# Attention with a mixture-of-experts feed-forward on one core: row maxima issued by a table, and other units for the small work

## The reference, cut to what matters

```python
x = x + tanh(g_xattn) * xattn(layernorm(x), ctx, ctx)      # scores * 0.125, softmax over 1601 keys
x = x + tanh(g_ffn) * moe(layernorm(x))                    # 8 experts, top 2 per token
```

## Time and profile before

| | |
|---|---|
| median of 3 runs | 1453.89 us (1453.78 to 1454.77) |
| profiled execution | 1453.8 us, span 1452.0 us |
| PE, DVE, ACT, POOL busy, share of the span | 94%, 81%, 76%, 38% |
| first window of maxima, first score | 25.7 us, 46.2 us |
| attention ends, first expert matmul | 1259.6 us, 1264.3 us |

### The profile page before, as it was taken

How to read it: one execution, slowest core, us unless ns; L and a number is a source line. 1 busy time by engine, 2 the same in 40 slices (tenths; PEclk the granted TensorE clock), 3 DMA queues, 4 the chain that set the end, 5 groups by cost and what they waited for, 6 DMA issues and landing times.

```text
span 1452.0 us, 37914 instructions
## 1 busy us (share of the span) xinstructions
PE 1357.7 (94%) x13936; PEld 643.2 (44%) x13936; DVE 1175.5 (81%) x2300; ACT 1102.6 (76%) x2202; POOL 549.6 (38%) x1214
## 2 busy tenths in 40 slices
PE   4699999999999999999999999999999999899992
PEld 2134444444343444443434343434343444488882
DVE  6578898989898989898998989898989899355334
ACT  1278888888888888888888888888888888765551
POOL 2241535252534353534434343435252511145442
PEclk7599999999999999999999999999999999999996
DMA  4321121212120212121211212121211110276665
GB/s 138 91 79 56 37 69 39 72 34 77 31 81 25 71 38 67 46 62 51 57 57 53 60 52 62 49 63 45 67 40 47 38 46 2 67 228 208 197 196 207
DMA packets 65540, 109.15 MB, mean 75 GB/s; under 512 B 13436, under 2 KB 36348, under 8 KB 65212
## 3 DMA queue, kind: packets, MB, share of 16 engines
q1 hardware_dynamic: 56572, 91.64, 21.4%
q0 software_dynamic: 4544, 9.45, 1.9%
q10 hardware_dynamic: 4240, 5.65, 1.3%
HBM read 48.81 MB, written 14.64 MB: 44 GB/s over the span
## 4 chain that ended last, share of the span: by engine, by line
PE 61%; DVE 25%; SPq 5%; issue 3%; DMA 2%; POOL 2%; ACTq 0%; ACT 0%; POOLq 0%; DVEq 0%
DVE mx L1437 20%; PE pv L738 20%; PE mxp L717 11%; PE st L695 10%; PE st L968 5%; PE mxp L976 5%; SPq L364 4%; PE st L797 3%; PE st L806 3%; PE st L817 1%; DMA arena<-results 1%; PE st L840 1%; DMA qpack<-mxT 1%; PE mxp L947 1%; PE mxp L955 1%
## 5 line engine op out<-in xcount | busy, mean ns | idle before, releaser
L1437 DVE TENSOR_REDUCE mx<-mxp 128x2 f32<-128x804 f32 x1024 | 982.9, 988 | 126.2 <-PE mxp L717 113.7
L1005 ACT ACTIVATE arena<-st 128x512 f32<-128x512 f32 (+1 forms) x1664 | 897.9, 594 | 124.3 <-PE st L695 114.3
L738 PE MATMUL pv<-arena 128*32 128x256 f32 x6656 | 536.0, 394 | 0.5
L695 PE MATMUL st<-qpack,kpack 51*128 51x256 bf16 (+1 forms) x3328 | 464.4, 274 | 11.6 <-ACT kf L1036 8.9
L717 PE MATMUL mxp<-kpack,qpack 48*128 48x402 bf16 x2048 | 437.8, 345 | 34.5 <-DVE mx L1437 30.6
L695 PEld LDWEIGHTS st<-qpack,kpack 51*128 51x128 bf16 (+1 forms) x3328 | 209.5, 97 | 166.6 <-ACT arena L1005 56.2
L717 PEld LDWEIGHTS mxp<-kpack,qpack 48*128 48x128 bf16 x2048 | 128.0, 94 | 252.9 <-DVE mx L1437 136.2
L738 PEld LDWEIGHTS pv<-arena 128*32 128x32 f32 x6656 | 132.7, 109 | 178.0 <-issue 119.5
L1147 ACT ACTIVATE arena<-st,bias 128x256 f32<-128x256 f32 x156 | 73.6, 473 | 63.6 <-PE st L968 60.9
L633 POOL DMA_INDIRECT results<-ysb,idx x78 | 74.7, 957 | 93.4 <-DVE ysb L1576 80.3
L968 PE MATMUL st<-xT,arena 128*128 128x256 f32 x312 | 95.7, 390 | 4.5 <-issue 2.6
(11 more groups left out here) (182 smaller groups left out, 1075.0 us busy)
## 6 DMA issues: line engine op xcount, KB each, us to landing
kpack<-ksp SPq DMA_DIRECT2D x762, 50.0 KB
arena<-in_ctxT SPq DMA_DIRECT2D x14, 800.5 KB, 4.5
arena<-in_w1T SPq DMA_DIRECT2D x39, 256.0 KB
arena<-in_w2T SPq DMA_DIRECT2D x39, 256.0 KB
qpack<-qsp SPq DMA_DIRECT2D x186, 32.0 KB
xblk<-rows SPq DMA_DIRECT2D x39, 132.0 KB, 2.8
rows<-in_pads SPq DMA_DIRECT2D x8, 264.0 KB, 3.7
qpack<-mxT SPq DMA_DIRECT2D x128, 3.0 KB
```

The source lines that it names most:

```text
L695: ins = eng.matmul(ring[i][0:n, jj * N:(jj + 1) * N], kpack[rows, b % 2, g * JJ + jj, kt * P:kt * P + n], qpack[rows, b % 2, g * JJ + jj, ...
L738: ins = eng.matmul(pv[32 * j:32 * j + 32, 0:N], vaug[0:n, b % 2, kt, VC * h:VC * h + 32], pt[0:n, (2 * u + rg) % PT_BUFS, jj * N:(jj + 1) ...
L1005: eng.activation(pt[0:n, c % PT_BUFS, :], ring[bank_of["S", u, p]][0:n, :], ACT.Exp, scale=SCALE).then_inc(s_exp, 1)
L1437: eng.tensor_reduce(mx[:, tj, w, :], mxp[windows_done % MX_BUFS][:, :, 0:WIN], AX.X, ALU.max).then_inc(s_red, 1)
```

## The change

Windows of maxima are issued by a written table: `WINDOWS_AT` says for each of the 52 units how many stand in the scores (first string, 35) and at the end (second string, 29), 64 a batch as before. The windows run 29 ahead (before 27), but only 20 are issued ahead of the first score (before 22), and the lead is made up over the first 27 units. `small` goes by the unit: routing has one step a unit from r = 29 (before two steps at each of ten maxima), the X norm has one step at the end of each of the units 28 to 32, the L norm one in each of 11 to 15. Nearly all units of the tables move. At the start POOL's memset of the whole of `vaug` goes; DVE sets the columns of ones and the padding instead. SP packs group 2 of batch 0 ahead of `place_maxima(0)`, and ACT's queue packs group 3. POOL splits the maxima of groups 3 and 4 ahead of what stood before them.

```diff
-AHEAD = KT + 9
-SHORT = 4
-K_AT = {2: 0, 5: 1, 10: 2, 11: 3}
-V_AT = {19: 0, 20: 1, 28: 2, 32: 3}
-HEADS_AT, TURN_AT, PLACE_AT = {4: 0, 18: 1, 31: 2, 44: 3}, {8: 1, 22: 2, 34: 3, 48: 4}, {9: 1, 23: 2, 35: 3, 49: 4}
-POST_AT = {7: "C", 9: "F", 24: "L", 27: "R"}
-X_AT, Q_AT = 36, 42
-X1_AT, Q1_AT = 4, 7
-RANK_AT, LAST_RANK_AT, COUNT_AT, PLAN_AT = 43, 40, 42, 44
+K_AT = {1: 0, 3: 1, 7: 2, 11: 3}
+V_AT = {14: 0, 26: 1, 27: 2, 32: 3}
+HEADS_AT, TURN_AT, PLACE_AT = {2: 0, 22: 1, 29: 2, 41: 3}, {8: 1, 21: 2, 34: 3, 47: 4}, {9: 1, 22: 2, 35: 3, 48: 4}
+POST_AT = {6: "C", 10: "F", 23: "L", 25: "R"}
+X_AT, Q_AT = 36, 40
+X1_AT, Q1_AT = 4, 6
+RANK_AT, LAST_RANK_AT, COUNT_AT, PLAN_AT = 46, 35, 38, 40
+L_NORM_AT, X_NORM_AT = 11, 28
+LOGITS_AT, EXP_AT, ROUTE_AT = 26, 28, 29
+LEAD, SHORT = 29, 9
+WINDOWS_AT = ("1101110001111100111001011111011010011111010011110111",
+              "0110012110100120001111100111010011100001111000110000")
...
+def issued(u, p):
+
+    b, r = divmod(u, UNITS)
+    return LEAD + b * PER_BATCH + ISSUED[2 * r + p] - max(0, SHORT - u // 3)
...
@@ SP
+            pack_keys(0, 2)
             place_maxima(0)
-            for g in range(2, NG):
-                pack_keys(0, g)
@@ POOL
             norm("X", 0)
-            eng.memset(vaug, 1.0).then_inc(s_vone, 1)
             split_maxima(0)
...
+                split_maxima(b * NG + 3)
                 if b + 2 < B:
                     norm("X", b + 2)
-                split_maxima(b * NG + 3)
+                if b + 1 < B:
+                    split_maxima(b * NG + 4)
                 if b > 0:
                     count_first(b - 1)
@@ ACT
             eng.dma_start(ctx_sb[:, 1, :], ctxT[1]).then_inc(s_ctx[1], 16)
+            for part in range(PARTS):
+                for rg in range(RG):
+                    pack_key_rows(eng, 0, NG - 1, part, rg)
@@ DVE
-            def small(b, w):
+            def small(b, r, p):
+
+                if p == 1:
+                    if b + 2 < B and X_NORM_AT <= r < X_NORM_AT + 5:
+                        norm_step("X", b + 2, r - X_NORM_AT)
+                    return
...
+                each = 4 if last else 1
+                first = r - (rank_at(b) + 1)
...
+                for n in range(each * (r - ROUTE_AT), each * (r + 1 - ROUTE_AT)):
+                    if 0 <= n < 20:
+                        routing_step(b - 1, n)
...
+            eng.memset(vaug[:, :, :, 0:VC * H].rearrange("p k t (h c) -> p (k t) h c", c=VC)[:, :, :, DH], 1.0
+                       ).then_inc(s_vone, 1)
+            eng.memset(vaug[:, :, :, VC * H:VW].rearrange("p k t w -> p (k t) w"), 0.0).then_inc(s_vone, 1)
...
-            for v in range(AHEAD - SHORT):
-                for p in range(RG):
-                    for w in windows(v, p):
-                        maximum(*w)
-                if KT <= v:
-                    norm_step("X", 1, v - KT)
+            for n in range(issued(0, 0)):
+                maximum(*divmod(n, NMX))
+            for n in range(5):
+                norm_step("X", 1, n)
...
+                for w in windows(u, 0):
+                    maximum(*w)
+                small(b, r, 0)
...
+                for w in windows(u, 1):
+                    maximum(*w)
+                small(b, r, 1)
```

More of the change, by code:

```diff
@@ L86 @@
 N_W2 = 4
-K_AT = {2: 0, 5: 1, 10: 2, 11: 3}
-V_AT = {19: 0, 20: 1, 28: 2, 32: 3}
-HEADS_AT, TURN_AT, PLACE_AT = {4: 0, 18: 1, 31: 2, 44: 3}, {8: 1, 22: 2, 34: 3, 48: 4}, {9: 1, 23: 2, 35: 3, 49: 4}
-POST_AT = {7: "C", 9: "F", 24: "L", 27: "R"}
-X_AT, Q_AT = 36, 42
-X1_AT, Q1_AT = 4, 7
-RANK_AT, LAST_RANK_AT, COUNT_AT, PLAN_AT = 43, 40, 42, 44
-SLOTS = GROUPS * NMX // B
+K_AT = {1: 0, 3: 1, 7: 2, 11: 3}
[10 more added lines that the diff above has]
+              "0110012110100120001111100111010011100001111000110000")
+PER_BATCH = NG * NMX
+ISSUED = [sum(int(WINDOWS_AT[q][r]) for r in range(UNITS) for q in range(2) if 2 * r + q < c)
+          for c in range(2 * UNITS)]
 def key_rows(kt):
     return min(P, M - kt * P)
+def issued(u, p):
+    b, r = divmod(u, UNITS)
+    return LEAD + b * PER_BATCH + ISSUED[2 * r + p] - max(0, SHORT - u // 3)
 def windows(u, p):
[L103 to L113, removed]
+    to = issued(u, 1) if p == 0 else issued(u + 1, 0)
+    return [divmod(n, NMX) for n in range(issued(u, p), min(to, GROUPS * NMX))]
 def rank_at(b):
@@ L891, in _ @@
                 b, r = divmod(u, UNITS)
-                first = [w for v in beside(u) for w in windows(v, 0)]
-                scores(u, 0, first[:1])
+                scores(u, 0, windows(u, 0)[:1])
                 scores(u, 1, [])
-                for w in first[1:]:
+                for w in windows(u, 0)[1:]:
                     maximum(*w)
@@ L931, in _ @@
                     count_tokens(0)
-                for v in beside(u):
-                    for w in windows(v, 1):
-                        maximum(*w)
+                for w in windows(u, 1):
+                    maximum(*w)
             for v in range(B * UNITS - LAG, B * UNITS):
@@ L1126, in _ @@
                             copy_tokens(b - 1)
-                    if r == 31:
+                    if r == EXP_AT:
                         exp_logits(b - 1)
@@ L1411, in take_full @@
                                              ALU.min).then_inc(s_dve, 1)
-            def small(b, w):
-                last = b == B - 1
[L1416 to L1424, removed]
+            def small(b, r, p):
[3 more added lines that the diff above has]
+                    return
+                if b == 0:
+                    return
+                last = b == B - 1
+                each = 4 if last else 1
+                first = r - (rank_at(b) + 1)
+                if L_NORM_AT <= r < L_NORM_AT + 5:
+                    norm_step("L", b - 1, r - L_NORM_AT)
+                elif LOGITS_AT <= r < LOGITS_AT + 2:
+                    logit_step(b - 1, r - LOGITS_AT)
+                for n in range(each * (r - ROUTE_AT), each * (r + 1 - ROUTE_AT)):
+                    if 0 <= n < 20:
                         routing_step(b - 1, n)
[L1426 to L1429, removed]
+                for n in range(1 + each * first, 1 + each * (first + 1)):
+                    if 1 <= n < 5:
+                        place_step(b - 1, n)
             def maximum(G, m):
```

7 lines of the change are left out of this document (2 added, 5 removed).

## The result

The changed kernel takes 1461.56 us in the median of 5 runs (1459.28 to 1462.2), the kernel before 1454.76 beside it (1453.78 to 1457.39): ratio 1.0041 [1.0026, 1.0055], **slower by 0.4%** where 1416 was forecast. The profiled execution has 1459.28 us and a span of 1457.2; that of before had 1452.0.

The account below looks back on a forecast made before the run. PE's unit work was put at 70.8 of 75.05 us a batch, 4.3 being stalls behind close second windows. Gains of 14 (start), 19 (batches 1 to 13), 3.2 and 1.2 summed to 37.4 off 1453.8: 1416 us, range 1388 to 1434.

Parts of the forecast that it names:

- One moved step is late: Steady batch: X norm's last step moves to unit 32, so PE waits 1.8 us for its rows in unit 36.
- rival A: Steady batches: the wait for the X rows does not come, 25 us more gained, 1391 us; chance 0.2.
- (d): Start: with continuous work TensorE stays at 2.4 GHz from about 49 us; about 18.5 gained by unit 9.
- What is left ... I take 1.1: Steady batch: stalls remaining at close second windows, turned maxima and backlog, 1.1 us a batch, bounds 0.5 and 3.
- Rival C: Steady batches: the table paces only half as well, stalls 2.8 instead of 1.1 us, 1440 us; chance 0.09.
- (a): Start: with POOL's memset gone, the packs and the first window come 3.65 us earlier.
- (c): Start, unit 2: ACT's 12.25 us wait for packs, and some 9 us of PE standing with it, go.
- (b): Start: group 2 packs before the first placing, group 3 on ACT; first score at about 42.1 instead of 46.2 us.
- rival B: Start: DMA engines, not issue, set it, so it brings 4, 1426 us; sign: first score after 44; chance 0.1.
- (e): Batch 0: second placing waits for queries ready near 64.4 us, lands at 89; a 4 to 5 us stall, 15.2 remain.
- The last batch: Last batch and hand-over: stalls fall 1.8, hand-over gains 2.3, PE stands 2.9 for divide; net 1.2 gained.
- rival D: Steady batches: X wait of 5 us behind a DVE backlog uses up the gain, 1461 us, slower; chance 0.04.

Follow-up runs that it names:

- e1: Changed kernel with the rows of batch b+2 turned in unit 38, not 36: 1411.87 us, ratio 0.9723 to the kernel before.
- e5: Changed kernel with rows turned in unit 38, plan behind unit 44 and packs of group 2 behind the first placing: 1406.09 us, ratio 0.9679.
- e18: e5 with one window moved from the end of unit 46 to the end of unit 3: 1410.98 us, ratio 0.9719.
- e6: Changed kernel with rows at 38 and the written table replaced by the even pattern from before: 1455.91 us, ratio 1.0011.
- e7: Changed kernel with rows at 38 and routing two steps at a time in units 34 to 43: 1417.66 us, ratio 0.9753.
- e8: Changed kernel with rows at 38 and three start edits (GpSimd memset, VectorE memsets, packs of groups 2 and 3) taken back: 1421.16 us, ratio 0.9771.
- e4: Changed kernel with SyncE's packs of group 2 behind the placing of the first maxima: 1454.42 us, ratio 1.0011.
- e3: Changed kernel with the last batch's plan steps behind unit 44, not 40: 1455.3 us, ratio 1.0014.
- e15: The changed kernel itself, run again in a series with the stand: 1519.56 us, ratio 1.0172.
- e9: Changed kernel with rows turned one unit earlier, in 35: 1570.97 us, ratio 1.0503.
- e11: e5 with one window moved from the end of unit 46 to the end of unit 3: 1492.45 us, ratio 0.9973.
- e12: Changed kernel with rows turned in unit 35, run once more: 1566.05 us, ratio 1.0448.
- e14: e5 with the window of unit 46 moved to unit 3, run again in a series with the stand: ratio 0.994.
- e17: e5 with the window of unit 46 moved to unit 3, in the series of e15: 1488.53 us, ratio 0.9955.
- the three edits: Changed kernel with rows in 38, plan behind 44, packs behind the first placing: 0.9679 as e5; 1486.6 us, 0.9948 in the series with the stand.

## Why the prediction was wrong, by its own steps

**The steady batch, "One moved step is late": this is the step that failed.** Place, releaser, number and length of the wait were right (14 times, 1.87 against 1.8, rival A's 1391 was never near). But the step was priced at the wait alone: "Sum: 70.7 + 1.1 + 1.8 = 73.6". The runs give 1.87 for the wait and, on average, 19.9 / 13 = 1.5 for the stretches at 1.2 GHz behind it, missing from the sum. The text had the low clock as a consequence of stands in batch 0 (step (d) of the start) and didn't carry it to its own new wait, nor to the 2.9 us stand that it put into the last batch. Over 14 batches that is some 21 us of the 45 between forecast and result.

**"What is left ... I take 1.1"** was mis-sized. Without wait a batch takes 72.77 (e1, e5), so stalls are 2.1 on a sum of 70.7 and not 1.1, within the bounds of 0.5 and 3. The two largest are unit 46 (2.41 in e5, against 1.59 by the prediction's own prices) and unit 2 (2.28 against 1.61); the prediction's list has a part of the first and not the second. This is 1.0 in each of 13 batches, 13 us. The first can't be had by moving its window alone (e18); the second was not tried. Rival C (1440) named 2.8, of the right kind but too much. That the even pattern costs 3.0 more (e6) bears out the reading of the earlier trace rows: second windows close behind the first were the stalls. That two routing steps at a time cost much, which the text drew from the 1.19 of the earlier trace rows, does not hold: 0.3 a batch (e7).

**The start** was put at 14 and brings 6 to 7 (mark of batch 1, e8). (a) is right in kind and too large: the memset is gone and the first window runs 2.0 us earlier (23.67 against 25.70), not 3.65. (c) is right: the 12.25 us wait is gone, and back in e8. (b) failed: the first score at 49.4 and not 42.1, because the packs, issued ahead of the placing "where SP waits anyway", were costed at their issue alone, and not at what they hold up behind them; e4 shows it. Against (b) the text had set what the Trainium skill, page "DMA: Bandwidth & Descriptors", section "Issuing engines are not separate DMA queues", says of shared DMA engines, and had chosen the sequencer. Each was right in part: the 12.25 us wait did go, and the first score was later than 44, the sign of rival B. (d) came late, with the full clock from about 55 us and not 49. (e) was too early by 7.8: the queries waited for GpSimd until 72.16, the placing landed at 97.5 and not at 89, and PE stood 0.6 us for it and not 4 to 5, since it was late itself.

**The last batch**: 2.9 us for `divide` were put down, 1.83 are the wait, and with the clock of 0.64 behind it the stretch is 3.4 longer. With the plan at 44 (e3) 3.1 of these come back, but the stretch is still 0.3 above that of before, so the 1.8 forecast from fewer stalls isn't there either. From the last copy to the first expert multiplication it is 2.22 us instead of 4.72: 2.5 gained, 2.3 forecast. That number is luck. The forecast had it from the plan four units earlier, and with the plan back at 44 it is 2.40 (e3) and 2.22 (e5); what does bring it was not tried.

Batch 14 (3.2 against 2.9) was right. Of the chance of 0.05 for slower, 0.04 went to rival D, a wait above 4.5 us. That its 1461 is the measured time is chance: the wait was 1.87 and not 5, and none of what D asks for happened. Its bound was worked out right: 37.4 / 14 + 1.8 a batch. Wait and clock together are 3.4 us a batch; with 8 less at the start, 1.0 more of stalls a batch and 2.5 less at the end, that was enough.

## What to carry to other kernels

A new wait of TensorE is priced with what the clock does behind it: here 0.8 and 1.25 us cost no more than themselves, 1.87 us cost 1.5 more on average, and 2.9 us 2.3 to 2.6 more; so work out each wait that an edit adds to some tenths, and move the consumer by a unit before the producer is tuned. A small transfer that something waits for goes ahead of the bulk, even where the queue would stand idle meanwhile: here that was 5.8 us at the first score and 3.6 behind batch 0. And where the stalls that are left all go back to one engine that is busy nine tenths of the time, moving the work that shows a stall may only move the stall.

## What the runs showed of the hardware that was not expected

- TensorE's clock fell to 1.2 GHz behind 11 of 14 stands of 1.87 us in an otherwise busy stream, and behind none of 14 at 0.8 and of 13 at 1.25. Which of the 14 keep it differs from trace to trace: the same waits in e3, e4 and e15 have the fall 12, 11 and 7 times, in other batches. The times of e3 and e4 spread over 13 and 17 us in 12 runs each, but those of the changed kernel itself over 3 in 5, so the spread alone shows little.
- In three series (e9 to e11, e12 to e14, e15 to e17) PE, ScalarE and VectorE stop together in unit 1 of each batch, where GpSimd scatters rows and SP packs queries. In e11 the unit takes 5.73 us (671.14 to 676.87; 1.94 in e5), and the releaser is none of this core's engines:

```profile
675.68 0.60 ACT L1000 ACTIVATE arena<-st 128x512 f32<-128x512 f32 x1 [2.54 <-remote]
675.89 0.99 DVE L1439 TENSOR_REDUCE mx<-mxp 128x2 f32<-128x804 f32 x1 [2.32 <-remote]
```

  Instructions last as long as elsewhere. SP's twelve packs of queries take 7.90 us to issue, as in e5. What stops the three is open; no run here looks into it. The series of e1 to e4 and that of e15 to e17 have the same chip number, 6, and only the second has the stand, so the chip alone doesn't decide it. The low clock follows this stand too, and the gain of the three edits shrinks from 3.2% to 0.5%. It isn't the same for all: in the series of e15 to e17 the kernel before has some 40 us more than beside the result, the changed kernel 58 and the three edits 80. The kernel before itself was not profiled in those series, and why the fastest loses most was not tried.
